# A two-block transformer kernel: attention's probability-times-value products made for two steps in a row

## What is computed

```python
scores = jnp.einsum('bhqd,bhkd->bhqk', q, k) / math.sqrt(hd)
scores = jnp.where(causal, scores, -jnp.inf)
att = jax.nn.softmax(scores, axis=-1)
out = jnp.einsum('bhqk,bhkd->bhqd', att, v)
```

## Time and profile before

| what | us |
|---|---|
| median of 3 runs | 624.41 |
| lowest and highest of them | 623.15, 629.63 |
| the profiled execution, device time | 620.05 |
| its span, from first to last instruction | 618.3 |
| what lies around the span in it | 1.75 |
| groups 0 to 7 of the attention, from the first product with values on | 384.69 to 606 |

### The profile page before, as it was taken

One profiled execution on the slowest core, in us unless ns is written; L12 is line 12 of the kernel. 1 busy time (PEld: TensorE's weight loads), 2 busy tenths in 40 slices (PEclk: granted clock), 3 DMA queues, 4 the chain that ended last, 5 costly groups with the idle time before them and its releaser, 6 DMA issues.

```text
span 618.3 us, 9492 instructions
## 1 busy us (share of the span) xinstructions
PE 597.6 (97%) x3758; PEld 398.9 (65%) x3758; DVE 373.7 (60%) x554; ACT 293.2 (47%) x513; POOL 77.1 (12%) x106
## 2 busy tenths in 40 slices
PE   7899999999999999999999999899999999999996
PEld 6688888877888887777677765444444444444444
DVE  5776645137644324885755446668898888871225
ACT  3655424124523222522212114777787677776772
POOL 3000000000000000502311112121112112121210
PEclk9999999999999999999999999899999999999999
DMA  5614242211120112377914743261616340101003
GB/s 174 203 69 136 69 130 74 102 35 65 39 69 34 52 51 64 89 191 213 170 58 139 138 137 69 49 114 29 120 44 103 78 65 27 24 17 31 16 12 137
DMA packets 24068, 53.14 MB, mean 86 GB/s; under 512 B 8384, under 2 KB 8896, under 8 KB 24016
## 3 DMA queue, kind: packets, MB, share of 16 engines
q1 hardware_dynamic: 23736, 51.96, 32.6%
q0 software_dynamic: 288, 0.58, 0.3%
HBM read 39.63 MB, written 10.60 MB: 81 GB/s over the span
## 4 chain that ended last, share of the span: by engine, by line
PE 83%; DVE 8%; ACT 6%; DMA 2%; issue 2%; SPq 0%; DVEq 0%; ACTq 0%
PE bank L1332 12%; PE bank L1315 10%; PE slot L1012 9%; PE bank L1012 9%; PE slot L1014 8%; PE slot L1013 8%; PE bank L1014 8%; PE bank L1013 8%; PE slot L1226 6%; ACT probs L995 4%; PE slot L1234 2%; DMA x_sb<-in_x 1%; PE slot L1315 1%; DMA stage<-in_stream 1%; DVE maxcol L1685 1%
## 5 line engine op out<-in xcount | busy, mean ns | idle before, releaser
L995 ACT ACTIVATE probs<-bank 128x512 f32<-128x512 f32 (+2 forms) x294 | 144.3, 567 | 47.6 <-PE bank L1315 44.1
L1685 DVE TENSOR_REDUCE maxcol<-slot 128x2 f32<-128x1024 f32 (+2 forms) x112 | 124.9, 1142 | 29.7 <-PE slot L1226 15.0
L1012 PE MATMUL slot<-xt_hi,ring_hi 128*128 128x512 f32 (+3 forms) x248 | 96.4, 389 | 4.0 <-DVE h_lo L1585 1.8
L1014 PE MATMUL slot<-xt_hi,ring_lo 128*128 128x512 f32 (+3 forms) x248 | 95.9, 387 | 0.0
L1013 PE MATMUL slot<-xt_lo,ring_hi 128*128 128x512 f32 (+3 forms) x248 | 95.8, 386 | 0.0
L1332 PE MATMUL bank<-probs,v_sb 128*32 128x512 f32 (+3 forms) x768 | 83.2, 507 | 0.1
L1315 PE MATMUL bank<-qst,kst 50*128 50x512 f32 (+3 forms) x275 | 72.7, 422 | 6.0 <-ACT probs L995 4.2
L1315 PEld LDWEIGHTS bank<-qst,kst 50*128 50x128 f32 x275 | 32.8, 188 | 60.5 <-ACT probs L995 56.0
L787 POOL TENSOR_SCALAR_AFFINE_SELECT probs<-probs 128x512 f32<-128x512 f32 x64 | 41.7, 651 | 181.3 <-ACT probs L995 181.3
L1685 DVE TENSOR_REDUCE maxrest<-slot 128x2 f32<-128x768 f32 (+3 forms) x48 | 49.9, 1046 | 19.7 <-PE slot L1234 19.5
L1226 PE MATMUL slot<-kst,qst 48*128 48x512 f32 (+3 forms) x288 | 56.8, 388 | 0.3 <-DVE maxcol L1685 0.3
(11 more groups left out here) (221 smaller groups left out, 862.9 us busy)
## 6 DMA issues: line engine op xcount, KB each, us to landing
stage<-in_stream SPq DMA_DIRECT2D x43, 512.0 KB, 3.5
qst<-heads_dram SPq DMA_DIRECT2D x12, 256.0 KB, 5.1
kst<-heads_dram SPq DMA_DIRECT2D x12, 256.0 KB, 7.7
heads_dram<-attn_hi SPq DMA_DIRECT2D x4, 512.0 KB
heads_dram<-attn_lo SPq DMA_DIRECT2D x4, 512.0 KB
out_y<-x_sb SPq DMA_DIRECT2D x8, 256.0 KB, 2.1
stage<-u_sb SPq DMA_DIRECT2D x56, 32.0 KB, 2.0
stage<-den_dram SPq DMA_DIRECT2D x14, 128.0 KB
```

What stands on the lines that cost most here:

```text
L995: act.activation(probs[:, to:to + heads, 0:n], score_ps(b)[:, 0:heads * n].rearrange("p (h n) -> p h n", n=n), ACT.Exp, scale=HD ** -0.5). ...
L1012: pe.matmul(out_ap, a[0], b[0], start=start, stop=False)
L1014: return pe.matmul(out_ap, a[1], b[0], start=False, stop=stop)
L1685: dve.tensor_reduce(per_head[:, :, slots[0]:slots[-1] + 1], scores, AX.X, ALU.max).then_inc(S["max_free"], 1)
```

## The change

For steps up to step 3 of group 6 the products with the probabilities are no longer made one step at a time, two steps late. An even step now makes the products of the two steps before it, one right behind the other; an odd step makes none. So an even k is weighed at k + 2 as before and an odd k at k + 1. Both halves (4 and 8 steps) end with a pair, so that no pair spans two halves. From step 4 of group 6 on (`SINGLE_FROM` is 76, counted over all groups) single products stay at k + 2. ACT's `take_u` moves one step earlier in the paired part, to step 5 and to step 1 of the next group.

```diff
+SINGLE_FROM = STEPS * (GROUPS - 2) + MAX_END + 1
+
+def weighed_after(i):
+
+    if i >= SINGLE_FROM:
+        return [i - LAG]
+    return [i - 2, i - 1] if i % 2 == 0 and i > 0 else []
+
+def taken_before(g, half):
+
+    last = STEPS * g + (HT, STEPS)[half] - 1
+    return 1 + next(i for i in range(STEPS * GROUPS) if last in weighed_after(i))
...
-                    if s == HT + LAG:
+                    if STEPS * g + s == taken_before(g, 0):
                         take_u(g, 0)
-                    if s == LAG and g > 0:
+                    if g > 0 and STEPS * g + s == taken_before(g - 1, 1):
                         take_u(g - 1, 1)
...
-                        k = STEPS * g + s - LAG
-                        if hh == GH - 1 and k >= 0:
-                            weigh_values(k)
+                        if hh == GH - 1:
+                            for k in weighed_after(STEPS * g + s):
+                                weigh_values(k)
```

## The result

The changed kernel takes 631.12 us in the median of 15 runs (625.75 to 638.35), the kernel before 623.93 beside it (15 runs): ratio 1.0119, 95% interval 1.0086 to 1.0151. It is slower by 7.2 us between the medians, 7.4 by the ratio. Ratios and their intervals here compare fast runs alone (those within 1.5% of the fastest run of the same kernel), while medians are over all runs. The profiled execution of the changed kernel took 630.43 us, with a span of 628.7 against 618.3.

A forecast was written before the change was run, and what follows sets the result against it. PE's order was taken to bound the kernel (busy 97% of the span). Six groups' +4.0 us of ring waits less saved round trips, and -0.34 for the 37th, gave +3.6 on the 624.41 median: 628.0 us, range 617 to 634.5.

The forecast's parts named there:

- the 1% bound: A change of about 6.2 us, what a measurement can tell from none; slower by more was given 0.28.
- the forecast's own range: 624 to 631.5 us, given a chance of 0.55.
- The change of shape: On PE between scores and products: each pair saves one round trip of 0.34 us, 12.6 us over 37 pairs without waits.
- The walk through the six pairs: Per group, scores waiting for exponentials lose 2.7 us and round trips save 2.04, net +0.66 us.
- the signs: If right: PE's busy share down, recorded waits for exponentials from 4.6 us to over 10, step 8's second score at 1.4 to 1.5.
- 6 x 0.66 = +4.0: The walked group's net loss of 0.66 us taken for six cycles of six pairs, 36 of the 37 pairs.
- The 37th round trip: -0.34: Steps 3 and 4 of group 6, with a ring of five banks: 0.34 us saved with nothing lost.
- the ring: Three score banks: a score waits for the exponential of three banks before; without the product's cover six pairs lose 2.7 us.
- rival C: PE's new waits bring falls of the granted clock, 1.4 us each; four more falls give 633.6 us; chance 0.20.
- Rival A: The cover between steps isn't needed and round trips are saved in full: -12.6 us, 611.8; chance 0.10.
- B: The ring holds, but half of the 2.7 us is regained by overlap and DVE catching up: -4.5, 619.9; chance 0.15.

The follow-up runs named there:

- pairs_narrow: The changed kernel with pairs made only in steps 4, 8 and 10, all other products single; ratio 1.0100 to the kernel before.
- short_max_pairs: The changed kernel with DVE's reductions over half of the columns; 621.17 us, against 615.87 us for the kernel before with the same short reductions.
- pairs_wide_first: The changed kernel with pairs made only in steps 0, 2 and 6, the other products single and one step late; ratio 1.0129 to the kernel before.
- units_first_narrow: The changed kernel with the maxima behind the second score in steps 4, 8 and 10 moved behind the first; 620.59 us, ratio 1.0004 to the kernel before.
- before_again: The kernel before, unchanged, run as a kernel of its own to get each run's granted clock; 623.12 us, ratio 0.9955.

## Why the prediction was right, and where it fell short

Forecast: 628.0 us, +3.6. Measured: 631.1, +7.2 between the medians, beyond the 1% bound and at the upper edge of the forecast's own range. The direction and the mechanism came out; the size was half of what came.

- The change of shape. Pairs of 512 and 256 columns take 1.43 instead of 1.57, as in the working (0.12 + 0.02).
- The walk through the six pairs. From the first score of a pair to its products I had 3.1, 4.1, 3.5, 2.4, 3.83 and 2.75. In group 4 it is 3.17, 3.94, 3.60, 2.40, 3.88 and 2.73 (3.96 - 0.79, 5.58 - 1.64, 5.03 - 1.43, 3.61 - 1.21, 5.73 - 1.85, 4.37 - 1.64). Group 4 is +0.64 for the +0.66 of the sum, and the second score of step 8 is at 1.48 for 1.47. The single pairs are off by up to 0.16, and that their sum is right to 0.04 is in part luck. The recorded waits of scores for exponentials went from 4.6 to 8.6 us and not to over 10, as the signs had it.
- What failed in size is "6 x 0.66 = +4.0". I walked one group and took it for all. In the groups of the other kind the pairs cost 0.87. The difference lies in the last two pairs, steps 11 to 2. From the product in step 10 to that in step 2, first before (groups 4 and 5), then after:

```profile
515.82:525.74 9.92, 9.24 (x80) 4.05 (x79) 8.76 (x9) 7.86 (x17) 1.90 (x3) 1.00 0.05 15
543.45:553.58 10.13, 9.46 (x80) 3.94 (x79) 8.68 (x9) 7.26 (x16) 2.19 (x3) 1.00 0.04 15
```

```profile
525.66:535.32 9.66, 9.06 (x79) 4.48 (x78) 8.90 (x10) 7.83 (x17) 1.66 (x3) 1.00 0.09 23
553.92:564.03 10.11, 9.58 (x79) 4.31 (x78) 8.99 (x9) 7.44 (x16) 1.67 (x3) 1.00 0.07 20
```

  These pairs save 0.26 us in group 4 and 0.02 in group 5; the four in front of them cost 0.9 in both.
- The term "The 37th round trip: -0.34" did not come. I had it that steps 3 and 4 of group 6 lose nothing because the ring has five banks there. But the code lets the first three banks of the wide ring wait as in a ring of three (L1303, `b < WIDE_FROM + RING`), and the trace after shows that wait, 0.97 behind the first score of step 3 at 565.67:

```profile
566.64 0.77 PE L1331 MATMUL bank<-qst,kst 50*128 50x512 f32 x2 [0.25 <-ACT probs L1011]
```

  From the first product of group 6 to the end both kernels take the same (618.3 - 553.58 = 64.7, 628.7 - 564.03 = 64.7). Without this term, and with both kinds of groups, the sum is 3 x 0.64 + 3 x 0.87 = 4.5, and 4.7 +- 0.2 were measured at full clock (619.4 - 614.7).
- The clock, rival C, is probably the larger part of the miss (2.4 +- 1.0 us, where 1.1 is missing at full clock). I gave it 0.20 as an alternative, with 5.6 us for four falls. It came beside the forecast. That PE's waits bring the falls, as the rival says, no run shows: pairs_narrow has more waits than the changed kernel and 20.6 us at the lower level for 28.8. The price of a fall was too high as well: group 3 is of the kind of group 5, so it is 29.06 - 27.84 = 1.2 and not 1.4. And the kernel before itself spends 22.8 us at the lower level in an average run, of which its profiled execution showed two stretches and a short one at its end.
- Rival A (full saving, 611.8) and B (half regained, 619.9) did not come; PE's busy time did go down in the undisturbed groups, from 26.81 to 26.41, as the prediction's signs had it.
- That the ring and not DVE decides holds for the change as made (short_max_pairs), though the two are close: where the pairs' surroundings are changed, DVE's slot ends the waits (pairs_wide_first, units_first_narrow).
- Said of this kernel's order: the price of the pairs was PE's strict queue. The units of maxima that could have filled the wait stood behind the score that waited.

## What to carry to other kernels

Work that stands between two uses of a small ring of buffers is cover, even if it is put there for nothing of the kind: before merging it with its neighbour to save a fixed price, work through the consumer's latency from the first use to the reuse. Where a wait appears in an in-order queue, look first for independent work that stands behind the waiting instruction and can be put in front of it; here one number in a table gave back 5.7 us. And walk each kind of a repeating group, not one.

## What the runs showed of the hardware

- The time at the lower clock level differs from run to run of one kernel: spans of the changed kernel's first 15 runs go from 624.0 us at a mean clock of 0.989 to 636.6 at 0.964. The slope is 0.37 us for each us at that level there and 0.43 in before_again. Taking every run to full clock brought the standard error of a mean over 12 runs down to 0.2 to 0.4 us, and differences of 1 us became visible.
- Kernels with the same work in another order spend from 14.7 to 31.5 us of a run at the lower level, on average. units_first_narrow has 14.7 +- 1.3 where the kernel before has 22.8 +- 1.4 over all its runs and 22.1 +- 3.3 beside it; what makes the difference isn't settled.
- A change of PE's shape costs 0.10 to 0.12 us on each side, here between 50-row scores, 128-row products in 32 columns and 128-row, 128-column products; between equal shapes matmuls of 512 columns follow at 0.23 us.
